# TensorE's order in attention: both score pairs of a key tile first, then two maxima, the value product, two maxima

## The chip, the cores and the metric

The kernel runs on one core of one Trainium2 chip. The metric is the device time of a run in microseconds (us). Before the change the median of 3 runs is 499.24 us (498.36 to 499.49). All times below are us unless marked ns.

## The reference

Input x is 2 batches of 512 tokens with 128 features; a condition vector per batch modulates four layers that follow one another: a gated linear recurrence with ternary weights (L0), a transformer block with full attention (L1), a masked feed-forward block (L2) and a transformer block with causal attention (L3). The change touches the two attentions alone:

```python
# L1 (no mask) and L3 (causal), 16 heads of 8 features, 512 tokens, 2 batches
scores = einsum("bhqd,bhkd->bhqk", q, k) * hd ** -0.5      # L3: -inf above the diagonal
attn = softmax(scores, axis=-1)
out = einsum("bhqk,bhkd->bhqd", attn, v)
x = x + gate * (out.reshape(b, t, c) @ w_proj + b_proj)
```

## The kernel before, in words

Attention works in 8 **units** of 4 heads each: unit u is batch u // 4, head group u % 4. For each unit the kernel needs the maximum of every row of scores, then the exponentials, then their product with the values. A query or key is held as a stack of bf16 pieces in 64 rows; the heads of even and of odd number lie in rows 0 to 63 and 64 to 127, and so two matmuls of neighbouring heads use different rows of TensorE's array.

Five engines take part, and each one works through its own list in order:

- **Maxima.** TensorE multiplies queries by keys into one bank of PSUM (line 1431; in the causal attention a mask matmul, line 1428, goes ahead), and VectorE reduces the bank to a negated maximum (line 926). In the full attention a unit has 16 such items of 512 columns, in the causal attention 12 of several widths. They are written M0, M1, ... here. The banks form a **ring** of three (`RING`), which all ring items share: item r waits until item r - 3 has been consumed (`consumed`).
- **Parts.** When the last maximum of a unit is reduced, GpSimd splits it into three bf16 parts (lines 429 to 432, four small instructions in a row), TensorE transposes them (ring item `parts`, line 1402, waits for the semaphore `nm3`), VectorE copies the result (line 931), and a DMA (line 329) puts it into the query stacks, where it subtracts the maximum in the score matmul.
- **Scores.** For each of the 4 **key tiles** kt of a unit TensorE computes the scores of 4 heads in two pairs (steps s = 2k and 2k + 1 of the loop, k = 4u + kt; line 1471, causal mask line 1467), each pair into one of two double banks E. ScalarE takes the exponential of each pair (line 1157) into P.
- **Value product.** `probs_out(u, kt)` (line 1445) multiplies the values by P for 4 heads, 8 float32 matmul instructions that accumulate over the 4 key tiles in bank 6. It runs one key tile late: the product of key tile k - 1 stands in the loop's turn k. The product of kt = 0, which stands in the turn of kt = 1, waits until ScalarE has copied the unit before out of bank 6 (`unit_out`, line 1132). ScalarE makes this copy between the two exponentials of kt = 1.
- **Out.** TensorE transposes the copied unit (ring item `out`, line 1407), and VectorE divides it (lines 941 and 942).

The maxima run ahead of the scores: in the turn k of unit u those of unit u + 1 are made. `schedule` deals the ring items out to 66 slots, one ahead of the loop and one behind each score pair. In the full attention, units 0 to 5 (and the first two turns of unit 6), a turn has:

```
kt = 0: slot 2k+1: M8, M9      slot 2k+2: M10, M11          (of unit u + 1)
kt = 1: slot 2k+1: M12, M13    slot 2k+2: M14, M15
kt = 2: slot 2k+1: M0, M1 (of unit u + 2), parts (u + 1)    slot 2k+2: M2, M3, out (u - 1)
kt = 3: slot 2k+1: M4, M5      slot 2k+2: M6, M7
```

In the causal attention slot 2k + 1 has two maxima and slot 2k + 2 one (kt = 1: M9, M10, then M11, the unit's last); parts and out stand in the same places. Behind turn 1 of unit 6 no maxima are left. In TensorE's list a turn is: score pair, slot 2k + 1, score pair, slot 2k + 2, value product of k - 1. A score pair waits for the exponential of the pair two steps before it (its double bank).

Of the kernel before, what the change touches and what calls it, by code (L numbers as in the profile page):

```python
# [57 lines left out]
def build(nc, x_in, out, wa_in, w0_in, w1_in, w2_in, w3_in, row0_in, rowa_in, rowg_in, col_in, mask_in, c_in, ident_in,  # L58
          cmask_in, inv_in, sel_in, fill_in):
    with ExitStack() as ctx:  # L60
# [5 lines left out]
        def sem(name):  # L66
            if name not in sems:
                sems[name] = ctx.enter_context(nc.semaphore(name))
            return sems[name]
# [9 lines left out]
        def stack_of(a, qk, b, h, lo, hi):  # L79

            row = 64 * (h % 2)
            return stacks[row:row + 64, a, qk, b, h // 2, lo:hi]
# [151 lines left out]
        EARLY = {52: "o_turn", 54: "proj", 60: "n_turn"}  # L234
        COPIED, MODULATED = 54, 62
        TURNS = [(n, b) for n, _, _ in SEQ for b in range(B) if b or n not in (1, 5)]
        MLP_NO = {n: i for i, n in enumerate(MLPS)}

# [3 lines left out]
        def schedule(n):  # L242

            maxima = [("max", u, i) for u in range(8) for i in range(n)]  # L250
            at, slots = 0, [[]]

            def advance(to):
                nonlocal at
                while at < min(to, len(maxima)):
                    slots[-1] += [(item, 1) for item in START[n].get(at, ())]
                    slots[-1].append(maxima[at])
                    at += 1
                    if at > n and at % n == LAG:
                        slots[-1].append(("parts", at // n - 1))  # L260

            ahead = n + n // 2
            first = 2 * n
            advance(min(first, ahead))
            last = 8 * (len(maxima) - ahead + 0) // n
            for s in range(64):
                slots.append([])
                advance(min(ahead + ((s + 1) * n + 7) // 8 - (0 if s >= 39 else 0), first + (s + 1) * n // 5))
                if s == last + 1:
                    slots[-1].append(("parts", 7))  # L270
                if s >= 8 and s % 8 == 5:
                    slots[-1].append(("out", s // 8 - 1))
                if s in EARLY:
                    slots[-1].append((EARLY[s], 0))
            slots.append([("out", 7), ("o_turn", 1), ("proj", 1), ("norm", 1)])
            return slots
# [172 lines left out]
        def _(dve):  # L449
# [128 lines left out]
            def clip(i0, i1):  # L578

                def f():  # L580
                    for i in range(i0, i1):
                        _, w, at, n, _ = PARTS[i]
                        dve.wait_ge(sem("rounded"), i + 1)
                        v.tensor_scalar(w[:, at:at + n], w[:, at:at + n], MAGIC + 1.0, MAGIC - 1.0, ALU.min,
                                        ALU.max).then_inc(sem("clipped"), 1)
                return f
# [376 lines left out]
        def _(act):  # L963
# [23 lines left out]
            def ternaries(i0, i1):  # L987
                for i in range(i0, i1):
                    _, w, at, n, to = PARTS[i]
                    act.wait_ge(sem("clipped"), i + 1)  # L990
                    s_.activation(tern[:, to:to + n], w[:, at:at + n], ACT.Identity,
                                  bias=magic[:, 1:2]).then_inc(sem("tern"), 1)
# [184 lines left out]
        def _(pe):  # L1177
# [185 lines left out]
            for n, kind, layer in SEQ:  # L1363
                if kind == "att":
# [11 lines left out]
                    slots = schedule(len(steps))  # L1376
# [60 lines left out]
                    def probs_out(u, kt):  # L1437

                        b, g = u // 4, u % 4
                        q0 = 128 * kt if causal else 0  # L1440
                        pe.wait_ge(sem(f"a{a}_p"), 2 * (TB * u + kt + 1))
                        if kt == 0 and u >= 1:
                            pe.wait_ge(sem(f"a{a}_pvs"), u)
                        for h in range(HG):
                            last = t_.matmul(bank[6][32 * h:32 * h + 32, q0:S], V[b][:, kt, HG * g + h, :],  # L1445
                                             P[:, kt % 2, h, q0:S], start=(kt == 0), stop=(kt == TB - 1),
                                             tile_position=(0, 32 * h))
                        last.then_inc(sem(f"a{a}_pv"), 1)
# [5 lines left out]
                        ring_item(*x)  # L1454
                    pe.wait_ge(sem(f"a{a}_split"), 4)
                    pe.wait_ge(sem(f"a{a}_vs"), 2)
                    for s in range(64):
                        u, kt, p = s // 8, s // 2 % 4, s % 2
                        b, g = u // 4, u % 4
                        q0 = 128 * kt if causal else 0  # L1460
                        if kt == 0 and p == 0:
                            pe.wait_ge(sem(f"a{a}_mrow{u % 2}"), 16 * (u // 2 + 1))
                        if s >= 2:
                            pe.wait_ge(sem(f"a{a}_p"), s - 1)
                        if causal:
                            for j in range(2):
                                t_.matmul(E[s % 2][:, j, q0:q0 + 128], cmask[:, 0], cmask[:, 2], start=True, stop=False,  # L1467
                                          skip_group_check=True)
                        for j in range(2):
                            h = HG * g + 2 * p + j  # L1470
                            last = t_.matmul(E[s % 2][:, j, q0:S], stack_of(a, 1, b, h, kt * 128, (kt + 1) * 128),  # L1471
                                             stack_of(a, 0, b, h, q0, S), start=not causal, stop=True,
                                             skip_group_check=causal)
                        last.then_inc(sem(f"a{a}_sc"), 1)
                        for x in slots[s + 1]:
                            ring_item(*x)
                        if p == 1 and s > 1:
                            probs_out((s - 2) // 8, (s - 2) // 2 % 4)
                    probs_out(7, TB - 1)
                    pe.wait_ge(sem("n_hT"), B * (n + 1) + 1)  # L1480
                    for c in range(4):
# [92 lines left out]
```

## Time and profile before

| | us |
|---|---|
| median of 3 runs | 499.24 |
| the profiled execution | 497.21 |
| its span, first to last instruction | 495.4 |
| TensorE matmuls busy (share of the span) | 341.1 (69%) |
| VectorE busy | 311.7 (63%) |
| ScalarE busy | 243.1 (49%) |
| mean granted TensorE clock | 0.847 |
| chain that ended last, TensorE's share | 51% |

The full attention's loop runs from about 196 to 294 us of the span, the causal one's from about 371 to 472 us. The page names engines PE (TensorE matmuls), PEld (its weight loads), DVE (VectorE), ACT (ScalarE), POOL (GpSimd) and SP. A row of a timeline merges instructions of one line that follow closely; a matmul's duration contains its latency, so the distance between the starts of two rows tells what a matmul costs the engine.

### The profile page before, as it was taken

The page shows a single profiled execution, that of the slowest core. Times are in us where ns is not written, and L with a number is a line of the kernel's source. Part 1 is how long each engine was busy: PE and PEld are TensorE (multiplying, and loading weights), DVE is VectorE, ACT ScalarE, POOL GpSimd, SP SyncE. Part 2 cuts the span into 40 slices and gives each one's busy share as a digit, 9 for nine tenths or more (in the row PEclk, how much of TensorE's full clock was granted, in tenths as well). Part 3 has the DMA queues.
Part 4 walks back from the last instruction along what each step waited for, and adds up shares of the span by engine and source line. Part 5 has one row for each costly group of instructions (what it writes and reads, how often), then busy time and mean ns, then how long its engine had stood idle before and what let it go on. Part 6 is the DMA issues. An engine that isn't in the chain of part 4 may idle for free.

```text
span 495.4 us, 5838 instructions
## 1 busy us (share of the span) xinstructions
PE 341.1 (69%) x1986; PEld 155.4 (31%) x1986; DVE 311.7 (63%) x787; ACT 243.1 (49%) x422; POOL 111.9 (23%) x177
## 2 busy tenths in 40 slices
PE   0025745521445377988888978758699999999886
PEld 0014513410124221122222325535322344434354
DVE  0778787869688669788888505255674655555230
ACT  3267566551564222666666774323503444445542
POOL 0112149622263410000000132363100000000410
PEclk9999955555557775799999999988856999999999
DMA  7940070000000421000000000000620000000001
GB/s 250 416 168 0 1 169 2 1 0 0 1 0 1 123 80 54 1 3 1 3 2 3 2 1 0 1 0 2 177 80 3 2 3 1 1 3 3 3 1 44
DMA packets 12139, 19.88 MB, mean 40 GB/s; under 512 B 2598, under 2 KB 11050, under 8 KB 11434
## 3 DMA queue, kind: packets, MB, share of 16 engines
q1 hardware_dynamic: 12108, 19.49, 12.5%
q8 instruction: 16, 0.26, 0.2%
q14 instruction: 15, 0.12, 0.1%
HBM read 12.41 MB, written 0.52 MB: 26 GB/s over the span
## 4 chain that ended last, share of the span: by engine, by line
PE 51%; DVE 24%; ACT 10%; POOL 7%; issue 5%; DMA 1%; SPq 0%; DVEq 0%; ACTq 0%; POOLq 0%
PE ps L1445 10%; PE ps L1431 10%; PE pe L1471 6%; DVE nm L926 5%; PE pe L1360 4%; PE ps L1503 4%; PE ps L1428 3%; PE pe L1467 3%; POOL rstd L343 2%; PE ps L1407 2%; DVE st L506 2%; ACT scr L1044 2%; PE ps L1231 1%; POOL xn L439 1%; DVE xn L516 1%
## 5 line engine op out<-in xcount | busy, mean ns | idle before, releaser
L926 DVE TENSOR_REDUCE nm<-ps 128x1 f32<-128x512 f32 (+2 forms) x224 | 135.6, 648 | 53.9 <-PE ps L1431 52.2
L1157 ACT ACTIVATE scr<-pe 128x1024 f32<-128x1024 f32 (+3 forms) x128 | 108.7, 864 | 100.5 <-PE pe L1471 100.5
L1431 PE MATMUL ps<-big 64*128 64x512 bf16 (+3 forms) x256 | 79.3, 378 | 11.7 <-DVE nm L926 11.7
L1445 PE MATMUL ps<-scr 128*32 128x512 f32 (+3 forms) x512 | 59.6, 538 | 4.4 <-ACT scr L1132 3.6
L343 POOL TENSOR_TENSOR rstd<-var,half 128x4 f32<-128x4 f32 x26 | 28.5, 1098 | 111.3 <-DVE var L511 86.7
L1471 PE MATMUL pe<-big 64*128 64x512 bf16 (+3 forms) x256 | 47.8, 361 | 0.5 <-ACT scr L1157 0.5
L429 POOL CAST nm<-nm 128x16 bf16<-128x16 f32 x16 | 3.1, 196 | 194.0 <-DVE nm L926 194.0
L1431 PEld LDWEIGHTS ps<-big 64*128 64x128 bf16 x256 | 19.3, 95 | 47.8 <-DVE nm L926 34.0
L1360 PE MATMUL pe<-hT,w 128*128 128x512 f32 x48 | 24.8, 642 | 3.5 <-ACT hT L1111 3.5
L1428 PE MATMUL ps<-cmask 128*128 128x128 bf16 (+1 forms) x96 | 25.1, 262 | 2.5 <-DMA big<-tern 1.2
L516 DVE TENSOR_SCALAR xn<-x_tok,mv,rstd 128x128 f32<-128x128 f32 x56 | 15.8, 345 | 13.5 <-POOL rstd L343 13.5
L1471 PEld LDWEIGHTS pe<-big 64*128 64x128 bf16 x256 | 12.4, 94 | 37.0 <-ACT scr L1157 18.4
L1170 ACT ACTIVATE scr<-pe,col 128x512 f32<-128x512 f32 x24 | 16.3, 688 | 14.6 <-PE pe L1360 14.6
L1467 PE MATMUL pe<-cmask 128*128 128x128 bf16 x128 | 18.8, 230 | 0.6 <-ACT scr L1157 0.6
L1231 PE MATMUL pe<-ident,xn 128*128 128x128 f32 x20 | 4.6, 372 | 20.6 <-ACT xn L1044 13.0
L955 DVE TENSOR_TENSOR x_tok<-x_tok,ps 128x512 f32<-128x512 f32 x6 | 4.1, 687 | 21.6 <-PE ps L1503 21.5
L941 DVE RECIPROCAL rec<-ps 128x16 f32<-128x16 f32 x16 | 4.0, 252 | 21.5 <-PE ps L1407 21.5
L1044 ACT ACTIVATE scr<-scr,magic,q 128x128 f32<-128x128 f32 x32 | 12.7, 480 | 9.4 <-DVE q L660 9.4
L1036 ACT ACTIVATE junk<-scr 128x128 f32<-128x128 f32 x24 | 7.1, 297 | 20.6 <-DVE scr L639 20.5
L1445 PEld LDWEIGHTS ps<-scr 128*32 128x32 f32 x512 | 10.4, 108 | 19.2 <-ACT scr L1157 11.2
L1231 PE MATMUL ps<-ident,scr 128*128 128x128 f32 x24 | 6.4, 431 | 14.5 <-ACT scr L1044 13.7
L1111 ACT ACTIVATE hT<-ps,modc 128x512 f32<-128x512 f32 x8 | 6.2, 776 | 20.4 <-PE ps L1231 20.3
(223 smaller groups left out, 595.6 us busy)
## 6 DMA issues: line engine op xcount, KB each, us to landing
big<-tern SPq DMA_DIRECT2D x48, 128.0 KB, 2.4
big<-in_wa SPq DMA_DIRECT2D x1, 2304.0 KB, 12.3
w<-in_w SPq DMA_DIRECT2D x2, 1152.0 KB, 19.1
big<-in_wa SPq DMA_DIRECT2D x1, 1344.0 KB, 6.0
big<-in_w SPq DMA_DIRECT2D x1, 1024.0 KB, 14.2
w<-in_w SPq DMA_DIRECT2D x1, 896.0 KB, 19.6
rowg<-in_rowg SPq DMA_DIRECT2D x1, 832.0 KB, 18.0
row<-in_row SPq DMA_DIRECT2D x1, 640.0 KB, 14.3
```

The costliest lines, as they stand in the source:

```text
L343: nc.gpsimd.tensor_tensor(dst, src, half[0:src.shape[0], 0:n], ALU.pow).then_inc(sem(done), 1)
L516: last = v.tensor_scalar(xn[:, t], x_tok[:, t], mv[:, t, 0:1], rstd[:, t:t + 1], ALU.subtract, ALU.mult)
L926: v.tensor_reduce(dst, src[:, 0:w * len(hs)].rearrange("p (h w) -> p h w", w=w), AX.X, ALU.max, negate=True).then_inc(sem(f"a{a}_max"), 1)
L1044: last = s_.activation(dst[:, t], src[:, t], ACT.Identity, bias=magic[:, 0:1], scale=q4[:, 3, m, t:t + 1])
L1157: s_.activation(P[:, kt % 2, 2 * p:2 * p + 2, q0:S], E[(e - 1) % 2][:, :, q0:S], ACT.Exp, scale=SCALE).then_inc(sem(f"a{a}_p"), 1)
L1360: t_.matmul(bank[2 + i % 4], m["w"][:, m["at"] + c * D:m["at"] + (c + 1) * D], hT[:, b], start=True, stop=True).then_inc(sem(f"n{n}_h"), 1)
L1428: t_.matmul(diagonal, cmask[:, 0], wide(cmask[:, 1], len(hs)), start=True, stop=False, skip_group_check=True)
L1431: last = t_.matmul(dst[:, k * wd:(k + 1) * wd], stack_of(a, 0, b, HG * g + h, qt * 128, (qt + 1) * 128), stack_of(a, 1, b, HG * g + h, 0, ...
L1445: last = t_.matmul(bank[6][32 * h:32 * h + 32, q0:S], V[b][:, kt, HG * g + h, :], P[:, kt % 2, h, q0:S], start=(kt == 0), stop=(kt == TB - 1),
L1467: t_.matmul(E[s % 2][:, j, q0:q0 + 128], cmask[:, 0], cmask[:, 2], start=True, stop=False, skip_group_check=True)
L1471: last = t_.matmul(E[s % 2][:, j, q0:S], stack_of(a, 1, b, h, kt * 128, (kt + 1) * 128), stack_of(a, 0, b, h, q0, S), start=not causal, st ...
L1503: last = t_.matmul(bank[6 + b][:, i * D:(i + 1) * D], hid[:, b, c, i * D:(i + 1) * D], gated_w(n, b, c), start=(c == 0), stop=(c == m["n"] ...
```

## The change

The loop over 64 score steps becomes a loop over 32 key tiles. In a turn TensorE now issues both score pairs, then the items of slot 2k + 1, then the value product of key tile k - 1, and then the items of slot 2k + 2. The instructions and their waits are the same ones; only TensorE's order changes.

```diff
-                    for s in range(64):
+                    def scores(s):
+
                         u, kt, p = s // 8, s // 2 % 4, s % 2
...
                         last.then_inc(sem(f"a{a}_sc"), 1)
-                        for x in slots[s + 1]:
+
+                    for k in range(32):
+                        scores(2 * k)
+                        scores(2 * k + 1)
+                        for x in slots[2 * k + 1]:
                             ring_item(*x)
-                        if p == 1 and s > 1:
-                            probs_out((s - 2) // 8, (s - 2) // 2 % 4)
+                        if k:
+                            probs_out((k - 1) // 4, (k - 1) % 4)
+                        for x in slots[2 * k + 2]:
+                            ring_item(*x)
                     probs_out(7, TB - 1)
```

## Rows read from the trace of the kernel before

**Rows 1.** Windows: length, busy PE, PEld, DVE, ACT, POOL, granted clock, DMA, GB/s.
```profile
201.00:207.00 6.00, 5.52 (x30) 1.10 (x31) 3.85 (x8) 2.36 (x3) 0.83 (x4) 0.76 0.01 3
...
231.00:243.00 12.00, 9.86 (x70) 2.69 (x69) 10.24 (x19) 8.35 (x9) 0.83 (x4) 1.00 0.01 1
...
310.00:325.00 15.00, 11.14 (x68) 8.01 (x68) 5.03 (x21) 5.61 (x9) 6.75 (x12) 1.00 0.00 1
325.00:340.00 15.00, 10.07 (x46) 6.46 (x45) 6.31 (x29) 3.94 (x6) 7.39 (x10) 0.77 0.00 0
...
400.00:440.00 40.00, 40.00 (x309) 16.25 (x309) 23.90 (x48) 19.82 (x29) 2.48 (x12) 1.00 0.01 2
```
**Rows 2.** Timeline, full attention, a turn kt = 0: start, length, engine, line [idle before].
```profile
234.07 0.39 PE L1471 MATMUL pe<-big 64*128 64x512 bf16 x2
234.29 0.38 PE L1431 MATMUL ps<-big 64*128 64x512 bf16 x2
...
234.71 2.48 DVE L926 TENSOR_REDUCE nm<-ps 128x1 f32<-128x512 f32 x4 [0.22 <-PE ps L1431]
...
235.46 0.39 PE L1431 MATMUL ps<-big 64*128 64x512 bf16 x1 [0.35 <-DVE nm L926]
...
235.77 1.07 PE L1445 MATMUL ps<-scr 128*32 128x512 f32 x8
...
236.77 0.39 PE L1471 MATMUL pe<-big 64*128 64x512 bf16 x2
```
**Rows 3.** Timeline, the next turn, kt = 1.
```profile
237.41 2.48 DVE L926 TENSOR_REDUCE nm<-ps 128x1 f32<-128x512 f32 x4 [0.22 <-PE ps L1431]
...
238.85 1.06 PE L1445 MATMUL ps<-scr 128*32 128x512 f32 x8 [0.30 <-ACT scr L1132]
...
239.84 0.39 PE L1471 MATMUL pe<-big 64*128 64x512 bf16 x2
```
**Rows 4.** Timeline, the turn after it, kt = 2, to the next score pair.
```profile
240.03 0.20 POOL L429 CAST nm<-nm 128x16 bf16<-128x16 f32 x1 [11.32 <-DVE nm L926]
...
241.22 0.22 PE L1402 MATMUL ps<-cmask,nm 128*64 128x128 bf16 x1 [0.78 <-DVE nm L926]
...
241.37 0.39 PE L1471 MATMUL pe<-big 64*128 64x512 bf16 x2
...
242.15 0.66 PE L1407 MATMUL ps<-ident,scr 128*128 128x128 f32 x4
...
242.73 1.06 PE L1445 MATMUL ps<-scr 128*32 128x512 f32 x8
243.22 0.25 DVE L941 RECIPROCAL rec<-ps 128x16 f32<-128x16 f32 x1
243.50 0.29 DVE L942 TENSOR_TENSOR xn<-ps,rec 128x128 f32<-128x128 f32 x1
...
243.73 0.39 PE L1471 MATMUL pe<-big 64*128 64x512 bf16 x2
```
**Rows 5.** Timeline, full attention, unit 7: two score pairs with nothing between.
```profile
282.78 0.61 PE L1471 MATMUL pe<-big 64*128 64x512 bf16 x4
```
**Rows 6.** Timeline, causal attention, kt = 1 and into kt = 2.
```profile
414.54 0.29 PE L1467 MATMUL pe<-cmask 128*128 128x128 bf16 x2
...
415.84 0.58 ACT L1132 COPY scr<-ps 128x512 f32<-128x512 f32 x1
...
415.99 0.28 PE L1467 MATMUL pe<-cmask 128*128 128x128 bf16 x2
...
416.63 0.39 PE L1431 MATMUL ps<-big 64*128 64x512 bf16 x1
416.95 1.06 PE L1445 MATMUL ps<-scr 128*32 128x512 f32 x8
...
417.88 0.20 POOL L429 CAST nm<-nm 128x16 bf16<-128x16 f32 x1 [11.65 <-DVE nm L926]
...
417.95 0.29 PE L1467 MATMUL pe<-cmask 128*128 128x128 bf16 x2
...
419.24 0.24 PE L1402 MATMUL ps<-cmask,nm 128*64 128x128 bf16 x1
```

**Rows 7.** DMA issues of the page: KB each, us to landing.
```profile
big<-tern SPq DMA_DIRECT2D x48, 128.0 KB, 2.4
```

## The prediction

> **What bounds the kernel now.** I read the granted clock and busy times by window first, then the timeline of both attentions in turns. In the windows [rows 1] the reader is to see two different stages. In the causal attention TensorE is busy for 40.00 of 40 us: it is the bound, in order, and a new wait there adds its whole length. In the full attention TensorE is busy for 9.86 of 12 us and VectorE for 10.24; neither is full, so the stage is bound by a chain between engines. Nothing else of the program is touched.
>
> The timeline gives that chain for a turn kt = 0 [rows 2]. Lengths are from start to start on TensorE: a score pair takes 0.22 (234.07 to 234.29), and so does a pair of maxima. M8 and M9 go out at 234.29, VectorE starts on M8 at 234.71 (0.42 later), and reduces four maxima in 2.48, 0.62 each. M11 needs M8's bank and goes out at 235.46, 0.75 behind the start of that reduction, after 0.35 of idle time. The product follows 0.31 later and takes 1.00. So the turn is 0.22 + 0.42 + 0.75 + 0.31 + 1.00 = 2.70, as measured (234.07 to 236.77). VectorE idles for 0.22 in it.
>
> In kt = 1 the product is later [rows 3]: the row names ScalarE's copy as releaser. From the score pair (236.77) to the product (238.85) is 2.08: exponential, then copy. With the 1.00 of the product the turn is 3.07 long (to 239.84).
>
> In kt = 2 the parts hold TensorE [rows 3, 4]. The reduction of M15 starts at 237.41 + 3 x 0.62 = 239.27; GpSimd starts 0.76 later (240.03), and the transposition 1.19 after that (241.22). The row puts the wait down to VectorE (a reduction that ends at that very time), but by the program the item behind M0 and M1 needs M15's bank and GpSimd's parts, and not M0: GpSimd is the releaser. The rest is score pair (0.15 after the parts), M2, M3, out, product (0.58 after out), to 243.73: a turn of 3.89. kt = 3 is like kt = 0. A unit is 2 x 2.70 + 3.07 + 3.89 = 12.36.
>
> **The change, full attention.** No instruction goes, none is added; the product moves ahead of slot 2k + 2, and the second score pair ahead of slot 2k + 1. I walk through the new order with the same intervals, with M10 of turn kt = 0 at time 0, right behind its product.
>
> - kt = 1. Score pairs 0.22 and 0.43 (two pairs with nothing between take no more: unit 7 issues four matmuls and has the next product 0.54 later [rows 5]). M12 0.65; M13 needs M10's bank: reduction at 0.42, plus 0.75 = 1.17. The product could start at 1.48, but the copy allows it only at 0.22 + 2.08 = 2.30. It ends at 3.30. Only now come M14 and M15, the last maxima of the unit, which stood ahead of it before. VectorE, done with M13 at 2.90, starts them at 3.72 and 4.34.
> - kt = 2. Score pairs 3.52 and 3.74, M0 3.95, M1 4.47 (M14's bank). GpSimd 4.34 + 0.76 = 5.10, parts 5.10 + 1.19 = 6.29. TensorE idles for 1.6 us here, and the product is queued behind the parts, as are M2, M3, out and the next turn. Product 6.46 (0.17 behind the parts: nearest row, parts to score pair 0.15 [rows 4]; a transposition to the product costs at most 0.58, and nothing is the least) to 7.46. M2, M3 7.46, out 7.78, next score pair 8.36.
> - kt = 3. M2 and M3 reduced from 7.88 and 8.50; then reciprocal and product of out (0.25 and 0.29 [rows 4]) until 9.72. M4 8.79; M5 needs M3's bank, 8.50 + 0.75 = 9.25; product 9.56 to 10.56; M6 10.56.
> - kt = 0. Score pairs 10.78, 11.00; M8 11.22; M9 needs M6: 10.98 + 0.75 = 11.73; product 12.04; M10 13.04. This turn is 2.48: VectorE's four reductions, with no idle time.
>
> A unit is 13.04 against 12.36: +0.68. The gain that the order offers is real in kt = 0 (2.48 for 2.70), but the last maxima of the unit are now behind a product that waits for the copy, and the next product is behind the parts, which wait for those maxima.
>
> The unknowns in it are how product and maxima follow each other at a new border: I took nothing between the product and M10, as between product and score pair now [rows 2], and 0.1 at most from the row of M11 to product (0.31 for a matmul of 0.22). Over four turns that is 0 to +0.4 a unit; below, a product ahead of maxima can save the 0.1 that M11 to product costs, twice in a unit where the wait hides it, -0.2. I keep +0.68 (-0.2 to +0.4).
>
> Unit 0 has no copy to wait for and its first turns are paced by VectorE at the half clock. There the product leaves 1.2 us earlier and VectorE's idle time, seen before as 3.85 busy of 6 us [rows 1], shrinks, while the parts come later; then two short turns follow. I take -0.6 up to turn 1 of unit 1 (-1.5 to +1). Five units from there: 5 x 0.68 = 3.4. Unit 6 has the late kt = 1 (3.30 for 3.07) and late parts, +0.6 together; behind that no maxima are left, unit 7 keeps its order, and the shift stays as it is. Full attention: -0.6 + 3.4 + 0.6 = +3.4.
>
> **The change, causal attention.** All of TensorE's blocks keep their length: each begins with a mask matmul over the full array in either order. Three blocks of score pair and two maxima take 1.45 (414.54 to 415.99), so a block is 0.48; M11 with its mask 0.48 too; the product 1.00 [rows 6]. Two waits appear.
>
> - Copy. It ends 1.88 behind the turn's start (415.84 + 0.58 - 414.54), and the product may start some 0.13 later (copy to product in the full attention), at 2.01. Before, five blocks lay ahead of the product (2.41), so the copy was hidden; now four, 4 x 0.48 = 1.93. New wait 0.08, units 1 to 6: 0.5.
> - Parts. M11's matmul leads GpSimd's start by 1.25 (416.63 to 417.88), and 1.19 more to the parts: 2.44, or 2.60 from M11's mask. Before, M11's last 0.32, the product and three blocks (1.29: 417.95 to 419.24) covered it. Now M11 stands behind the product: M11 0.48, two score pairs 0.43 each, M0 and M1 0.43 each, 2.20. New wait 2.60 - 2.20 = 0.40, units 1 to 5: 2.0. Unit 0's turn runs at the half clock, where the same blocks take more than the 2.60, and in unit 6 a product is ahead of the parts: nothing there.
>
> Bounds: if mask blocks can overlap more tightly behind each other the parts wait grows by 0.2 (+1.2); if POOL's start needs only what row 6 shows and TensorE's borders cost 0.1 more, it shrinks to 0.2 (-1.2). Causal attention: +2.5 (1.3 to 3.7).
>
> DMAs are neither moved on SP's queue nor added, but the row of maxima starts later. From parts to the next unit's first score pair were 2.51 + 2.70 = 5.2, and are 10.78 - 6.29 = 4.5; parts, copy and a landing of 2.4 (a piece eight times as large [rows 7]) fit. ScalarE keeps slack: exponentials, 1.9 for a pair of them, end before the bank is needed again 2.48 later.
>
> **Sum.** +3.4 + 2.5 = +5.9. Against the profiled execution's own 497.21: 503.1. That execution ran 2.03 under the median of 499.24; the predicted median is 499.24 + 5.9 = 505.1.
>
> **Rivals.**
>
> - B, only the full attention pays. In the causal one the two waits fit into slack that the 40.00 of 40 hides (ends of matmuls are modelled). +3.4: 502.6. For it: the waits are 0.08 and 0.40, near what the rows can tell. Against: the chain from M11 to the parts has only 0.17 of slack even now (417.88 + 1.19 = 419.07 against 419.24).
> - C, faster. The short turn is what decides: kt = 0 and kt = 3 fall to 2.48, in 13 turns, and kt = 1 and kt = 2 keep their length, since both start from a score pair that hasn't moved. -0.22 x 13 = -2.9: 496.3. It decides if the parts wait for M0's reduction, as the row of the parts literally says [rows 4], and GpSimd's chain is shorter than its rows: the parts would have to be ready 5.6 behind M10 (6.29 less the 0.68) to break even, and earlier still to win. Against: that chain is measured end to end in both attentions.
> - D, the clock falls. The longest idle stretch of TensorE in a unit grows from 0.78 to 1.6, and its busy share from 0.82 to about 0.78. The trace shows the full level, 2.4 GHz, granted at 11.14 busy of 15, and 0.77 of it at 10.07 of 15 [rows 1]; the new share is nearer to the first. If the level fell to 1.2 GHz for one unit, each product and matmul would double: some 1.0 + 4 x 0.22 per turn, of which VectorE's slack hides a part, about +5 per unit, so 508 to 515. The Trainium skill ("TensorE: Matmul & The Clock Gate", Part 1) tells that the slow clock is the default and that sustained activity releases it, so that idle time brings it back. By that rule the change is dangerous in its direction; the trace agrees that both levels occur, and shows none of the fall in this stage at gaps of 0.8.
> - E, no change: gain of short turns and loss of late parts cancel, within 1.0 of 499.24, for instance if kt = 3 too were 2.48 (-0.6 a unit) and the causal waits were hidden.
>
> **How the numbers follow.** The intervals reproduce the old order's turns to 0.01, so I give the forecast (501.5 to 508.5) 0.70, B 0.09, C 0.10, D 0.05, E 0.06. The forecast's bounds are full attention -0.6 - 0.2 x 6 and +1.0 + 0.4 x 6 at the extremes, causal 1.2 either way, not all at once. The range to hold 8 in 10 is 501.0 to 508.0. A measurement of this kernel tells 0.2% (1.0 us) from no change. Faster 0.10, same 0.06, slower 0.84.
>
> **What would show it.** In the profile after: turns kt = 0 of the full attention at 2.48 with VectorE at no idle time; turns kt = 1 with the product 2.08 behind the first score pair and VectorE idle for about 0.8 before M14; an idle stretch of 1.6 before the transposition of the parts (line 1402), with the product behind it; a unit of 13.0. In the causal attention an idle stretch of 0.40 before line 1402 and 0.08 before line 1445, where none was, and a unit of 13.2 for 12.7. The prediction is wrong if the parts don't wait longer than the 0.78 of now, if kt = 3 is as short as kt = 0, or if the clock of these stages falls below 1.00.

## The result, and the profile after

The changed kernel takes 519.84 us (median of 4 runs, 516.38 to 523.12) against 499.37 us before (498.36 to 499.78): ratio 1.0412, interval 1.0324 to 1.0501. The forecast was 505.1, range 501.0 to 508.0. The direction is right and the size is not: +5.9 forecast, +20.5 measured. The four runs are 516.38, 517.11, 522.57 and 523.12; the spread of 6.7 is itself something to explain, since the kernel before spreads by 1.4. The profiled execution took 516.38, span 514.5. The ratios here leave out runs that are over 1.5% above the fastest of the same kernel; since the clock makes just such runs here, single runs are given where they matter.

The waits of TensorE in the full attention come first (who waits for whom, total us, times, longest). The kernel after:

```profile
PE ps L1402 <- DVE nm L926: 8.7, 6, 1.5
PE ps L1445 <- ACT scr L1132: 4.4, 6, 0.7
```

The transposition of the parts (line 1402) waits for 1.49 in five units and for 1.26 in the first; it was 0.78 [rows 4]. The product (line 1445) waits 0.73 for the copy, and no maximum waits for its bank any more (it was 0.35 a turn [rows 2]).

The timeline of one unit after, from the product of kt = 0 on, answers to [rows 2 to 4] (columns as there):

```profile
239.10 1.06 PE L1445 MATMUL ps<-scr 128*32 128x512 f32 x8
240.10 0.39 PE L1431 MATMUL ps<-big 64*128 64x512 bf16 x2
240.32 0.59 PE L1472 MATMUL pe<-big 64*128 64x512 bf16 x4
...
242.39 1.06 PE L1445 MATMUL ps<-scr 128*32 128x512 f32 x8 [0.73 <-ACT scr L1132]
243.39 0.39 PE L1431 MATMUL ps<-big 64*128 64x512 bf16 x2
243.62 0.59 PE L1472 MATMUL pe<-big 64*128 64x512 bf16 x4
243.81 2.48 DVE L926 TENSOR_REDUCE nm<-ps 128x1 f32<-128x512 f32 x4 [0.81 <-PE ps L1431]
...
245.24 0.20 POOL L429 CAST nm<-nm 128x16 bf16<-128x16 f32 x1 [12.00 <-DVE nm L926]
...
246.43 0.22 PE L1402 MATMUL ps<-cmask,nm 128*64 128x128 bf16 x1 [1.49 <-DVE nm L926]
246.58 1.90 PE L1445 MATMUL ps<-scr 128*32 128x512 f32 x8
...
248.41 0.61 PE L1431 MATMUL ps<-big 64*128 64x512 bf16 x2
248.95 1.12 PE L1407 MATMUL ps<-ident,scr 128*128 128x128 f32 x4
```

With M10 at 240.10 as time 0, the walk of the prediction is there step by step: the score pairs at 0.22, the product at 2.29 (walked 2.30), M14 at 3.29 (3.30), GpSimd at 5.14 (5.10), the parts at 6.33 (6.29), the product 0.15 behind them. And then something that the walk doesn't have: that product takes 1.90 and not 1.06. The windows (from:to, length, busy PE, PEld, DVE, ACT, POOL, granted clock, DMA, GB/s) tell why:

```profile
245.00:246.00 1.00, 0.00 (x0) 0.00 (x0) 1.00 (x3) 0.97 (x2) 0.61 (x3) 1.00 0.00 0
246.00:247.00 1.00, 0.57 (x5) 0.27 (x9) 0.51 (x2) 0.00 (x0) 0.22 (x1) 0.84 0.00 0
247.00:248.00 1.00, 1.00 (x8) 0.00 (x0) 0.00 (x0) 0.00 (x0) 0.00 (x0) 0.50 0.00 0
...
250.00:251.00 1.00, 1.00 (x11) 0.47 (x14) 0.91 (x4) 0.54 (x1) 0.00 (x0) 0.96 0.00 0
```

TensorE stood still for 1.49, and its granted clock falls to half, 1.2 GHz, just as it starts again, for 3 to 4 us. From one transposition of the parts to the next, the units of the full attention take 12.37 before, and after 14.17, 13.05, 14.16, 13.05, 14.16 (starts 219.21, 233.38, 246.43, 260.59, 273.64, 287.80). 13.05 is the unit that the prediction walked (13.04); every second unit has a fall in it, 1.11 more. The two units between them have the same idle stretch of 1.49 at their start and no fall, so the stretch alone doesn't decide it.

The causal attention after, at its start, and then in its steady part:

```profile
376.00:396.00 20.00, 20.00 (x85) 5.57 (x84) 8.61 (x16) 5.47 (x8) 0.83 (x4) 0.50 0.01 2
396.00:413.00 17.00, 17.00 (x81) 4.47 (x80) 6.22 (x12) 5.13 (x7) 0.83 (x4) 0.50 0.01 1
...
414.00:416.00 2.00, 2.00 (x22) 0.88 (x20) 1.23 (x4) 0.76 (x2) 0.00 (x0) 1.00 0.00 0
```
```profile
437.75 0.22 POOL L432 TENSOR_TENSOR nm<-nmr,nm 128x16 bf16<-128x16 f32 x1
438.11 0.22 PE L1402 MATMUL ps<-cmask,nm 128*64 128x128 bf16 x1 [0.33 <-POOL nm L432]
438.25 0.85 PE L1445 MATMUL ps<-scr 128*32 128x384 f32 x8
```

The steady part is as walked: the parts wait for GpSimd (0.33; 0.40 walked), and a unit is 13.07 for 12.70. The start is not. There TensorE is busy without a gap and stays at half clock until 413.9 us, 38.3 behind the parts that stand ahead of the loop (375.65). Before, the same stretch at half clock ended at 381.4, 0.3 us ahead of the first parts in the loop and 14.3 behind those ahead of it (367.16):

```profile
367.50:381.00 13.50, 13.50 (x53) 3.62 (x52) 6.54 (x11) 4.02 (x5) 0.83 (x4) 0.50 0.01 1
...
381.00:382.00 1.00, 1.00 (x8) 0.43 (x6) 0.61 (x2) 0.24 (x1) 0.00 (x0) 0.79 0.00 0
...
382.00:400.00 18.00, 18.00 (x141) 7.16 (x139) 10.30 (x21) 7.75 (x13) 0.83 (x4) 1.00 0.02 4
```

From the first parts of that attention to the last I count the units: 14.55, 12.12, 12.70, then 12.7 before; 15.33, 19.47, 14.59, then 13.07 after. The steady units have the new wait for the parts (0.33) and none for the copy. The 19.1 us between the two spans are: 1.7 ahead of the attention (code that is the same; runs of the kernel before differ by as much among themselves), 6.8 in the full attention with its end, 0.8 + 7.35 + 1.9 in the first three units of the causal one, 1.5 in its others (three times 0.36, then 0.41), less 0.9 behind the last parts. So 3.3 of them are the three falls and 10.0 the late rise; the waits between the engines are the small rest.

### The profile page after: what moved, and what is told of

Its sections match the earlier page's. It is cut to its first block, busy times and chain, and to the rows that moved or that the text cites. A ratio compares the mean times of both kernels' runs of the same rounds, so it can differ in the third digit from the quotient of the medians.

```text
span 514.5 us, 5837 instructions
## 1 busy us (share of the span) xinstructions
PE 355.6 (69%) x1985; PEld 160.6 (31%) x1986; DVE 313.2 (61%) x787; ACT 240.1 (47%) x422; POOL 112.0 (22%) x177
## 4 chain that ended last, share of the span: by engine, by line
PE 49%; DVE 24%; ACT 11%; POOL 7%; issue 6%; DMA 1%; SPq 0%; DVEq 0%; POOLq 0%; ACTq 0%
PE ps L1445 10%; PE ps L1431 9%; DVE nm L926 5%; PE pe L1472 5%; PE pe L1360 4%; PE ps L1510 4%; PE ps L1428 3%; POOL rstd L343 2%; PE pe L1468 2%; PE ps L1407 2%; DVE st L506 2%; ACT scr L1044 2%; PE ps L1231 1%; POOL xn L439 1%; DVE xn L516 1%
## 5 line engine op out<-in xcount | busy, mean ns | idle before, releaser
L1157 ACT ACTIVATE scr<-pe 128x1024 f32<-128x1024 f32 (+3 forms) x128 | 106.3, 864 | 120.2 <-PE pe L1472 120.1
L1431 PE MATMUL ps<-big 64*128 64x512 bf16 (+3 forms) x256 | 80.5, 397 | 7.0 <-DVE nm L926 4.8
L1445 PE MATMUL ps<-scr 128*32 128x512 f32 (+3 forms) x512 | 64.9, 582 | 7.2 <-ACT scr L1132 6.2
L1472 PE MATMUL pe<-big 64*128 64x512 bf16 (+3 forms) x256 | 44.0, 371 | 0.7 <-ACT scr L1157 0.5
L1428 PE MATMUL ps<-cmask 128*128 128x128 bf16 (+1 forms) x96 | 26.2, 273 | 2.5 <-DVE nm L926 1.4
L1428 PEld LDWEIGHTS ps<-cmask 128*128 128x128 bf16 x96 | 9.5, 99 | 35.5 <-issue 22.2
L1044 ACT ACTIVATE scr<-scr,magic,q 128x128 f32<-128x128 f32 x32 | 12.7, 480 | 9.4 <-DVE q L660 9.4
```

What stands on the lines that cost most here:

```text
L1044: last = s_.activation(dst[:, t], src[:, t], ACT.Identity, bias=magic[:, 0:1], scale=q4[:, 3, m, t:t + 1])
L1157: s_.activation(P[:, kt % 2, 2 * p:2 * p + 2, q0:S], E[(e - 1) % 2][:, :, q0:S], ACT.Exp, scale=SCALE).then_inc(sem(f"a{a}_p"), 1)
L1428: t_.matmul(diagonal, cmask[:, 0], wide(cmask[:, 1], len(hs)), start=True, stop=False, skip_group_check=True)
L1431: last = t_.matmul(dst[:, k * wd:(k + 1) * wd], stack_of(a, 0, b, HG * g + h, qt * 128, (qt + 1) * 128), stack_of(a, 1, b, HG * g + h, 0, ...
```

## Experiments

Each kernel ran beside the kernel before, in 3 rounds, in three groups on the same chip each; the kernel before took 499.15, 498.76 and 498.4 (medians). All have the old and the new order only rearranged, or matmuls added whose results nobody reads. The edits are cut to the lines that differ between them. The order of a turn is chosen by one line, with these cases: `old` and `new` as before and after; `late` is score pairs, slot 2k + 1, slot 2k + 2, product; `parts_last` is score pairs, M0 and M1, product, parts, slot 2k + 2.

**full_only**

```diff
+mode = "old" if causal else "new"
```

> The new order in the full attention (L1), the old one in the causal attention (L3). Theory: late parts cost 0.7 a unit there (3.4 together), and the idle stretch of 1.5 us ahead of line 1402 drops the granted clock in some units, 1.1 each time, 3 to 4 of 6 units; the causal attention's long stretch at half clock belongs to the causal order and is gone. Then 499.4 + 3.4 + 4 = 505 to 509, causal parts(1) to parts(2) 12.1 as before. Rival: the full attention's order disturbs the clock of what follows, and the causal attention stays at half clock for 30 us and more with its old order too: 515 to 522.

505.98 (504.46, 505.17, 506.80, 506.93), ratio 1.0147 (1.0109 to 1.0186): +6.8, as expected. The units are 14.17, 13.05, 14.18, 13.05, 14.16, the same falls; the causal attention's first units are back at 14.56 and 12.12. So the long stretch at half clock comes with the causal attention's order.

**causal_only**

```diff
+mode = "new" if causal else "old"
```

> The old order in the full attention, the new one in the causal attention. Theory: two new waits, 0.36 a unit over 5 units, +2, plus a longer stretch at half clock at the start of the stage (+8 in the profile of the changed kernel), so 508 to 512, and more where it lasts longer. Rival (it comes from the full attention): 501 to 502, with the clock rising within 15 us of the stage's start as before.

507.63, 516.77, 517.30, 517.95: one run 0.4 below the 508 to 512 expected, three above it, where the expectation had only "more where it lasts longer". The profile is of one of 517.30. Its first units are 15.33, 19.47, 20.40, 14.59: the clock rises only at 427.9, at the start of the fourth.

```profile
385.00:404.00 19.00, 19.00 (x92) 5.06 (x85) 6.96 (x13) 5.90 (x9) 0.83 (x4) 0.50 0.01 2
404.00:427.00 23.00, 23.00 (x111) 6.86 (x110) 8.41 (x17) 5.91 (x9) 0.83 (x4) 0.50 0.01 2
```

A unit that misses the rise costs 7.3 us (19.47 for 12.12, 20.40 for 13.07), and the unit behind it, at whose start the clock rises, 1.5 (14.59 for 13.07). By its time the run of 507.6 has one late unit where the profiled one has two; of the 9.7 between them 7.3 is the second late unit, and 2.0 lies ahead of the causal attention in the profiled run (its parts ahead of the loop at 369.20, in the kernel before at 367.16). The changed kernel's spread is of the same kind: 516 to 517 with one late unit (its profile), and 522 to 523, which by this count have two. No trace of a run of 507.6 or of 522 to 523 is kept, so that is inferred.

**unit0_old and unit0_new**

```diff
+mode = ("old" if k < 4 else "new") if causal else "old"     # unit0_old
+mode = ("new" if k < 4 else "old") if causal else "old"     # unit0_new
```

> Full attention in the old order; causal attention: unit 0 in the old order, units 1 to 7 in the new one. Theory: the half clock lasts a unit longer because the new order in unit 0 keeps TensorE's clock from rising at kt = 2 of that unit; with unit 0 as before it rises there, and only the late parts cost, 0.36 a unit in 5 units, +2: 501.5 in all runs, parts(1) to parts(2) 12.1, later units 13.07. Rival: the new order in unit 1 and later matters for the clock too, or the rise is chance: runs of 508 and 517 appear as in causal_only.

> The opposite: causal attention with unit 0 in the new order, the others in the old one. Theory: late parts cost nothing in unit 0, so 499.5 in a run where the clock rises in unit 0, and 507 where it rises one unit later, at the old place; most runs of the second kind, and none above 509. Rival (clock independent of the order): 499 to 500 in nearly all runs.

unit0_old: nine runs from 499.23 to 501.79 and one of 510.20; ratio 1.0035 (1.0018 to 1.0053). unit0_new: 506.47, 507.07, 507.16, 509.13; ratio 1.0179 (1.0151 to 1.0206). Four turns in the new order at the start of the stage cost 8, and seven units in the new order behind them cost 1.4. The first late rise belongs to the order of unit 0: with the new order there all 12 runs are late (the changed kernel, causal_only and unit0_new), with the old one there 5 of 73 (the kernel before and all runs here without added matmuls in the causal attention, pairs_first left out), both by their times. Where unit 1 has the old order (unit0_new) none of four runs has the time of a second late unit, where it has the new one (causal_only) three of four have. The expectation for unit0_old had no late run in it; the one that came shows that chance has a part. It is the profiled run: units 14.68, 20.12, 14.76.

**pairs_first**

```diff
+mode = "late" if causal else "old"
```

> Full attention in the old order; causal attention with both score pairs first but both slots ahead of the product, so the product keeps its place at the end of the turn. Theory (the product ahead of slot 2k + 2 makes the parts late and moves the clock's rise): no new wait, clock rises as before, 499.2. Rival (pulling the second score pair ahead of the maxima does it): 501 and more, with runs of 507.

498.56 (ten runs, 497.03 to 500.17), ratio 0.9994 (0.9979 to 1.0009). Both score pairs in front cost nothing in the causal attention and leave the clock alone. This kernel differs from causal_only only in that the product stands behind slot 2k + 2; what does the harm there is the product ahead of that slot (M11 in kt = 1), with both score pairs in front. The product ahead of the slot without the score pairs in front was not run.

**filler and filler_half** (on top of full_only)

```diff
 if item == "parts":
+    if not causal and 2 <= u <= 6:
+        for _ in range(8):                      # filler_half: 3
+            t_.matmul(dst[:, 0:384], cmask[:, 0], cmask[:].rearrange("p k t -> p (k t)"), start=True, stop=True)
     pe.wait_ge(sem(f"a{a}_nm3"), u + 1)
```

> As full_only, with 8 matmuls of 384 columns on constants (into the bank that the parts then overwrite) ahead of the wait for the parts of units 2 to 6 of the full attention. They take about 1.3 of the 1.5 us that TensorE waits there. Theory (idle time drops the clock): the wait costs the same, the clock stays at the full level, units of 13.05 all, 1.1 less for each unit that fell in full_only: 503 to 504 for the whole. Rival (the clock falls for another reason, or the fillers only delay the parts): same as full_only or slower.

> As filler, with 3 matmuls of 384 columns in place of 8 ahead of the parts of units 2 to 6 of the full attention: they take about 0.5 us, and the idle stretch of 1.49 becomes one of about 1.0, close to the 0.78 that the kernel before has without a fall. Theory (the length of the idle stretch decides whether the clock falls): no fall, units of 13.05 all, 502. Rival (the clock falls by TensorE's busy share over the unit, whatever the length of one gap): some units of 14.2 remain, 503 to 505.

filler 501.77 (two of 8 runs at 511; the profile is of one of them, its causal units 14.67, 19.39, 12.70), ratio 1.0055 (1.0033 to 1.0078); filler_half 501.93 (one of 6 at 511.73), ratio 1.0062 (1.0040 to 1.0084); full_only was 505.98. More work on TensorE makes the kernel 4 us faster. The units are 13.21, 13.20, 13.20, 13.21 with eight fillers (0.15 too many of them) and 12.99 four times with three; none falls. The fillers take the falls away; they don't tell what brings them. They make the gap shorter and TensorE busier together: busy 10.38 of 13.05 us in a unit of full_only without a fall, 11.06 of 12.99 in filler_half, 11.80 of 13.20 in filler, and 10.23 of 12.37 in the kernel before, where nothing falls either. So the theory and the rival of filler_half, the length of one gap and the busy share of a unit, are not told apart. In full_only and in filler_half, the waits of TensorE in the full attention:

```profile
PE ps L1402 <- DVE nm L926: 8.7, 6, 1.5
```
```profile
PE ps L1406 <- POOL nm L432: 3.3, 6, 0.6
```

In filler_half 0.53 us of idle time is left ahead of the transposition in each of the five units with fillers, behind 0.5 of fillers and a wait of 0.21 for the bank. (The bank is waited for ahead of the fillers here, and the row of the parts names GpSimd, as the prediction had it.) The late parts alone cost 501.93 - 498.4 = 3.5, where the prediction had 3.4; the interval (1.0040 to 1.0084) makes that 2.0 to 4.2.

**dense_u0** (on top of unit0_new)

```diff
 if item == "parts":
+    if causal and u == 1:
+        for _ in range(12):
+            t_.matmul(dst[:, 0:384], cmask[:, 0], cmask[:].rearrange("p k t -> p (k t)"), start=True, stop=True)
```

> As unit0_new (507.1), with 12 matmuls of 384 columns on constants, full array, ahead of the parts(1) of the causal attention, where TensorE stands at half clock and has no idle time. At half clock they cost 12 x 0.32 = 3.8. Theory (at half clock the mix of matmuls decides whether the clock rises, and the product ahead of M11 breaks up the stretch that raised it): the clock rises at the fillers, and unit 1 takes 12.1 to 12.7 in place of 18.8: 507.1 + 3.8 - 6.5 = 504.4. Rival (the clock rises with time alone): 507.1 + 3.8 = 511.

501.88 (500.55 to 503.99), against 507.1 for unit0_new: 12 useless matmuls of 3.3 us save 5, 2.5 more than the 504.4 expected. Here TensorE had no idle time to fill. The trace shows them, and the clock:

```profile
384.63 0.39 PE L1435 MATMUL ps<-big 64*128 64x128 bf16 x2
384.95 3.34 PE L1403 MATMUL ps<-cmask 128*128 128x384 bf16 x12
388.22 0.24 PE L1406 MATMUL ps<-cmask,nm 128*64 128x128 bf16 x1
```
```profile
384.00:386.00 2.00, 2.00 (x10) 0.88 (x10) 0.85 (x2) 0.35 (x1) 0.25 (x2) 0.50 0.04 8
386.00:388.00 2.00, 2.00 (x10) 0.94 (x8) 0.00 (x0) 0.00 (x0) 0.00 (x0) 0.64 0.00 0
388.00:390.00 2.00, 2.00 (x18) 0.65 (x16) 0.40 (x2) 0.00 (x0) 0.00 (x0) 1.00 0.01 1
```

The clock is up at 387.5, before the last of them is through. The next unit takes 11.68 in place of 18.82, and the one behind it 12.71 in place of 14.36, which the expectation left out.

**best_full** (full attention only)

```diff
+mode = "old" if causal else ("new", "late", "parts_last", "new")[k % 4] if k < 26 else "old"
```

> Full attention: both score pairs first in all turns with maxima; in kt = 1 both slots ahead of the product (the last maxima not behind it), in kt = 2 the product ahead of the parts; kt = 0 and 3 as in the changed kernel. Causal attention as before. Theory (the last maxima of a unit and the parts set the loss): a unit of 11.2 in place of 12.37, no idle stretch over 0.8, clock at full level, 499.4 - 7 = 492.5. Rival (products behind a late copy set it, or both score pairs in front cost by themselves): 499 or slower.

492.61 (491.79 to 492.96), ratio 0.9884 (0.9847 to 0.9921): faster than both kernels. Four of five units take 11.17 or 11.18, one 11.36 (walked: 11.2). The waits of TensorE in the stage shrink to this:

```profile
PE ps L1431 <- DVE nm L926: 2.5, 12, 0.2
PE pe L1472 <- DMA big<-nmp: 0.5, 1, 0.5
```

The short turns that the change was able to give are all there, once the last maxima of a unit stand ahead of the product that waits for the copy, and the next product ahead of the parts. The two moves were made together; what each is worth was not measured. One wait for the DMA of the maxima (0.5, once, in the unit of 11.36) is new.

**best_warm and best_dense** (on top of best_full, in outline)

```diff
+if causal: warm_up(7)    # best_warm: ahead of the wait for the stacks, and again ahead of M3 of unit 0
+if causal: warm_up(12)   # best_dense: once, ahead of the first score pair
 # warm_up(n): n matmuls of 384 columns on constants into a free bank
```

> As best_full, with 7 matmuls of 384 columns on constants in each of two idle stretches of 1.24 us that TensorE has at the start of the causal attention (ahead of the wait for the first stacks, and ahead of maximum 3 of unit 0), into a bank that is free there. Their results are not used. Theory (idle stretches drop the clock, which stood at the full level there and at half from 361 to 381 us in the kernel before): the clock stays up through unit 0, 20 us at half become some 13 to 16 us: 488 to 490. Rival (the following maxima, paced by VectorE, drop it anyway): 492.6, as best_full.

> As best_full (492.6), with the same 12 matmuls ahead of the first score pair of the causal attention, into bank 6, which is free there. Theory: they cost 3.8 at half clock and raise the clock some 10 us earlier than now; unit 0's turns from there take half the time: -5, so 491.5, within 1 of best_full. Rival (they don't raise it): 496.5.

best_warm: 490.51, 492.30, 498.32, 498.95. Two runs gain up to 2 against the 492.61 of best_full, two lose 6. In its profile (498.95) the clock stays full until 360.3 us, over 8 us longer than in best_full (351.9), falls, and then misses the rise:

```profile
358.00:360.00 2.00, 1.93 (x9) 0.69 (x9) 2.00 (x4) 0.00 (x0) 0.00 (x0) 1.00 0.52 153
360.00:362.00 2.00, 0.76 (x6) 0.28 (x4) 1.38 (x4) 0.00 (x0) 0.82 (x4) 0.57 0.00 0
362.00:364.00 2.00, 2.00 (x8) 0.62 (x8) 0.91 (x2) 0.00 (x0) 0.00 (x0) 0.50 0.04 8
```
```profile
359.57 0.28 PE L1428 MATMUL ps<-cmask 128*128 128x256 bf16 x1
359.79 0.28 PE L1431 MATMUL ps<-big 64*128 64x128 bf16 x2
360.17 0.34 PE L1428 MATMUL ps<-cmask 128*128 128x256 bf16 x1
360.44 0.39 PE L1431 MATMUL ps<-big 64*128 64x128 bf16 x2
361.98 0.28 PE L1402 MATMUL ps<-cmask,nm 128*64 128x128 bf16 x1 [1.14 <-POOL nm L432]
```

This fall has no idle stretch ahead of it. The matmuls get longer at 360.17 and 360.44 already (0.34 for 0.28, 0.39 for 0.28), and the one wait, 1.14 for the parts of unit 0, begins behind them. In the 9 us before, TensorE was busy for all but 0.25, and its pauses were of 0.1. This is the rival of the expectation, in one trace.

best_dense: 490.70 (490.17 to 492.27), ratio 0.9856 (0.9825 to 0.9886), the lowest median here; its interval and best_full's overlap. Its 12 matmuls take 3.8 and the clock is up at 367.7, behind them, 7.0 after the parts ahead of the loop (best_full: 14.0). In the two profiles the time from those parts to the end of the span differs by 0.3 only (127.9 and 128.2): the early rise pays for the 12 matmuls and little more.

## Why the prediction was wrong

**Right, and near to the last digit:** the walk. A unit of 13.04 (13.05), idle time of 1.6 ahead of the parts (1.49), the product 2.08 behind the score pair (2.07), GpSimd and not VectorE as releaser. Unit 0 up to turn 1 of unit 1: -0.6 forecast, -0.65 measured (18.47 from its parts to that turn, 19.12 before). The full attention without its falls: 6.8 - 3.3 = 3.5, forecast 3.4. In the causal attention the wait for the parts came (0.33 for 0.40); the one of 0.08 for the copy shows in no row. Together they are 0.36 a unit in place of 0.48, 1.5 in all in place of 2.5. The waits between the engines were in the sum.

**The step that failed** is the sentence behind rival D, and with it the sum: the forecast took the granted clock of before as given, and put 0.05 on a fall "for one unit". It reasoned from the busy share of TensorE (0.82 to 0.78, against 0.67 where a lower clock was seen). That 0.67 was a poor guide: the granted 0.77 of that window is a mean of both levels, and the window has an idle stretch of 4.06 us in it. The runs show three falls in the five units with gaps of 1.49 (changed kernel and full_only), each of them 1.11, 3.3 together, and none once the gaps are filled (filler, filler_half). D's price, about 5 a unit, was too high: a fall lasted 3 to 4 us, not a unit. The sign that the prediction named for this case, a clock below 1.00 in these stages, is what came.

Would a closer look at the trace of before have told it? It has two idle stretches of nearly the same length, of which one (359.29; another of 1.24 ends 2.7 us ahead of it) is followed by a fall within 2 us, and one (319.62) is not followed by any for 10 us, though TensorE is busy for only 5.84 of the 10 from 320 on:

```profile
319.62 0.66 PE L1231 MATMUL ps<-ident,xn 128*128 128x128 f32 x4 [1.44 <-DVE xn L516]
359.29 0.28 PE L1428 MATMUL ps<-cmask 128*128 128x256 bf16 x1 [1.24 <-DVE nm L926]
```
```profile
320.00:330.00 10.00, 5.84 (x39) 4.34 (x37) 3.04 (x15) 3.64 (x5) 8.01 (x15) 1.00 0.00 0
360.00:362.00 2.00, 1.93 (x8) 0.67 (x7) 2.00 (x5) 0.00 (x0) 0.00 (x0) 0.73 0.70 200
```

So it could have told that a fall behind such a gap is possible, and worth more than 0.05, but not when it comes. In best_warm the fall at this same place came with the gaps filled.

**A second step** failed with more weight: "Unit 0's turn runs at the half clock, where the same blocks take more than the 2.60 ... nothing there." The arithmetic holds, and no wait appeared. But the sentence takes for granted that the stretch at half clock ends where it ended before. Counted from the parts ahead of the loop, it ended 24 us later (38.3 for 14.3), and in other runs a further unit later: 7.35 + 1.9 + 0.8 = 10.0 in the profile, by their times some 7 more in others. TensorE did the same matmuls, without a gap; only their sequence differed. No rival had this, since none asked what ends the half clock.

The Trainium skill ("TensorE: Matmul & The Clock Gate", Part 1) says that activity releases the throttle and idle time brings it back. The falls of the full attention agree with it in three units of five (1.49 idle, then 0.50 granted); the fall in best_warm, with no idle stretch ahead, doesn't. For the rise the trace agrees only in part: 37.00 of 37 us busy in the windows above, at 0.50 all along; in best_dense the clock is up 3.8 us behind the start of 12 full-array matmuls.

**Open.** Why the clock falls behind some gaps of 1.49 and not behind others, and which property of the sequence keeps it down in the causal attention. In the traces without added matmuls in that attention the rise came at kt = 2 or as that turn ended: 0.2 to 0.6 us ahead of the parts of the turn in the kernel before, full_only, filler, filler_half, pairs_first and best_full, and 3.5 to 4.0 behind them, at the end of the turn, in the changed kernel, causal_only, unit0_old and unit0_new. In the last the unit of the rise has the old order, so the order of that unit alone doesn't set the place. And chance has a part: one in ten runs of unit0_old, two of eight of filler, one of six of filler_half and one of the 41 runs of the kernel before (509.21) were late as well; two of these five are seen in traces, the others go by their times.

## What to carry to other kernels

Ask of every new wait two prices: its length, and what the clock does behind it. Here an idle stretch under 0.8 cost its length, and one of 1.5 another 1.1 in three units of five; filling it with useless matmuls gained 4 us. Where a stage starts at half clock, look at what stands ahead of the rise, in windows of 1 or 2 us: here the late rise cost 10 us and the new waits of the stage 1.5. And with items that feed a long chain (here the last maxima of a unit), put them ahead of whatever may wait for another engine, and things that wait for the chain behind what is ready: the same idea as the change, placed so, turned +1.5% in the full attention (full_only) into -1.2%.

## What was unexpected about the hardware

- The granted clock of TensorE fell behind gaps of 1.49 us in three of five units. Behind gaps of 0.78 (before) and 0.53 (filler_half) it didn't, nor behind one of 1.44 elsewhere in the kernel before. In one run (best_warm) it fell after 9 us in which TensorE was busy for all but 0.25.
- TensorE can be busy for 58 us without a pause, at half clock, before the clock rises (causal_only, 369.2 to 427.9). With the old order of the same matmuls the rise came 14.3 us behind the same parts (before).
- 12 matmuls of 384 columns over the full array were each time followed by the full clock within 3.8 us of their start, in both places where they were tried.
